# First expert stage in units of 256 rows, with stationary weights loaded for each unit

## The reference

```python
logits = xf @ Wg.T + bg                         # xf: layer norm of x, (4096, 256)
tp, ti = top_k(softmax(logits), 2)
tp = tp / (sum(tp) + 1e-8)
h = gelu(einsum('td,efd->tef', xf, W1) + b1)    # 8 experts, 256 -> 1024
y = einsum('tef,edf->ted', h, W2) + b2          # 1024 -> 256
x + einsum('ted,te->td', y, w)                  # w: tp at the two chosen experts
```

## Time and profile before

| | us |
|---|---|
| median of three runs | 1426.46 |
| the profiled execution's own time | 1424.49 |
| its span | 1422.7 |
| TensorE busy | 1353.1 (95%) |
| VectorE busy | 925.7 (65%) |
| ScalarE busy | 759.3 (53%) |
| GpSimd busy | 380.5 (27%) |
| first expert stage, first up product to the next stage's first product | 359.88 to 840.30 |

### The profile page before, as it was taken

One profiled execution on the slowest core, in us unless ns is written; L12 is line 12 of the kernel. 1 busy time (PEld: TensorE's weight loads), 2 busy tenths in 40 slices (PEclk: granted clock), 3 DMA queues, 4 the chain that ended last, 5 costly groups with the idle time before them and its releaser, 6 DMA issues.

```text
span 1422.7 us, 39700 instructions
## 1 busy us (share of the span) xinstructions
PE 1353.1 (95%) x14238; PEld 1164.5 (82%) x14238; DVE 925.7 (65%) x2570; ACT 759.3 (53%) x1734; POOL 380.5 (27%) x476
## 2 busy tenths in 40 slices
PE   7999999997899999999999989999999999899898
PEld 5888888885799999999999977889899898645476
DVE  4889999876555555555555545888888886412287
ACT  3666666562555555555555543565565655332353
POOL 1344444444030303031230013433344331100131
PEclk9999999997899999999999996999999999999999
DMA  5765445453321212122121111451111110399912
GB/s 185 278 221 171 158 156 171 143 184 118 138 98 38 105 38 97 43 101 97 43 101 39 38 50 38 174 188 47 46 47 57 50 39 17 129 390 428 357 63 67
DMA packets 95481, 175.98 MB, mean 124 GB/s; under 512 B 9024, under 2 KB 85568, under 8 KB 90688
## 3 DMA queue, kind: packets, MB, share of 16 engines
q1 hardware_dynamic: 88288, 144.09, 28.3%
q0 software_dynamic: 7008, 29.37, 6.0%
HBM read 112.87 MB, written 60.56 MB: 122 GB/s over the span
## 4 chain that ended last, share of the span: by engine, by line
PE 78%; DVE 13%; issue 3%; DMA 3%; ACT 2%; POOL 0%; SPq 0%; ACTq 0%; DVEq 0%; PEldq 0%; POOLq 0%
PE ps L1269 14%; PE ps L1254 7%; PE psS L519 4%; PE psS L1254 4%; PE ps L685 3%; PE psT L1254 3%; PE psT L528 3%; PE ps L545 3%; PE ps L551 3%; PE ps L640 3%; DVE arena L919 3%; PE ps L625 2%; PE ps L652 2%; PE psT L1237 2%; PE ps L1237 2%
## 5 line engine op out<-in xcount | busy, mean ns | idle before, releaser
L528 PE MATMUL psT<-arena 32*128 32x128 f32 x2048 | 151.5, 286 | 0.1
L519 PE MATMUL psS<-arena 32*128 32x256 f32 x1024 | 142.7, 397 | 0.7 <-ACT arena L797 0.7
L1269 PE MATMUL ps<-ring_hi,hT_hi 128*128 (+1 forms) x568 | 139.0, 283 | 0.4 <-ACT hT_hi L1282 0.4
L1269 PE MATMUL ps<-ring_lo,hT_hi 128*128 (+1 forms) x568 | 139.4, 283 | 0.0
L1300 ACT ACTIVATE arena<-arena 128x512 f32<-128x512 f32 x142 | 89.7, 632 | 77.1 <-DVE arena L1327 77.1
L1347 DVE TENSOR_TENSOR arena<-ps,arena 128x256 f32<-128x256 f32 x71 | 30.1, 424 | 154.0 <-PE ps L1269 154.0
L528 PEld LDWEIGHTS psT<-arena 32*128 32x128 f32 x2048 | 126.8, 189 | 1.2 <-issue 1.2
L1269 PEld LDWEIGHTS ps<-ring_hi,hT_hi 128*128 128x128 f32 x568 | 108.4, 191 | 3.4 <-issue 0.7
L1269 PEld LDWEIGHTS ps<-ring_lo,hT_hi 128*128 128x128 f32 x568 | 108.7, 191 | 2.7
L1282 ACT CAST hT_hi<-psT 128x512 fp32r<-128x512 f32 x71 | 41.7, 587 | 129.1 <-PE psT L1237 129.1
L919 DVE TENSOR_REDUCE arena<-psS 128x8 f32<-128x1024 f32 x64 | 78.4, 1224 | 44.6 <-PE psS L519 44.6
(11 more groups left out here) (295 smaller groups left out, 3686.7 us busy)
## 6 DMA issues: line engine op xcount, KB each, us to landing
arena<-wset_dram SPq DMA_DIRECT2D x24, 2048.0 KB, 15.2
xs_rows<-arena SPq DMA_DIRECT2D x32, 1024.0 KB, 5.9
arena<-w_dram POOLq DMA_DIRECT2D x6, 2048.0 KB, 9.0
w_sb<-xs_rows SPq DMA_DIRECT2D x71, 128.0 KB, 2.0
xs_rows<-arena SPq DMA_DIRECT2D x71, 128.0 KB, 1.7
arena<-ctxT_dram SPq DMA_DIRECT2D x63, 128.0 KB, 2.2
x_all<-x_dram SPq DMA_DIRECT2D x32, 128.0 KB, 2.1
arena<-w_dram SPq DMA_DIRECT2D x2, 2048.0 KB, 11.9
```

What stands on the lines that cost most here:

```text
L519: last = nc.tensor.matmul(psS[:, b, c * D:(c + 1) * D], qT[p, k % 3, c, :], kbd[p, k % 3, c, :, :], start=A, stop=A or c == 1, skip_group_ ...
L528: nc.tensor.matmul(psT[:, b, j * P:(j + 1) * P], kbd[p, (k - 1) % 3, c, par, :], qT[p, (k - 1) % 3, c, :], start=j == 0, stop=False, skip_ ...
L1269: last = nc.tensor.matmul(ps[5][:, 0:D], hp[:, f, :], wp[:, bass.ds(ring[j - 1], 1), o:o + D], start=n == 0 and f == 0 and wp is ring_hi, ...
```

## The change

The stage runs 33 units of 256 rows (pairs) and then 6 of 128 rows (singles). Routing makes the table in two parts: 33 pairs in `routing` and the six singles in `lone_units`, which VectorE runs in unit 1.

In a pair the weights are stationary and 256 tokens move, so that the up products come out transposed (1024 hidden features in eight groups of 128, two to a PSUM bank). ScalarE adds `b1` as the bias of gelu, straight from PSUM into `hid`. VectorE copies `hid` to `hT_hi` and subtracts into `hT_lo`, bank by bank. No hidden tile is transposed. Every pair loads its expert's weights, in two halves of 1 MB, into one of two slots; ScalarE rounds them in four pieces of 1024 columns between its gelus, and GpSimd subtracts in two instructions of 128x2048. `wb_lo` lies on the place of `wb_raw`. A single loads its weights whole (2 MB) into one of four places and multiplies in plain fp32: 16 up products of 128 columns and 8 down products of 256.

In `attention(0)` only expert 0's weights are prepared, in pieces of 256 columns (before: two experts, pieces of 512). The loads of `b1` to all partitions, the VectorE bias add, `cend_i`, and the reset of `vz` at the stage's end are gone; the context loads for `attention(1)` are issued at the start of the stage.

```diff
-UNITS = 2 * B + E0 - 1
-RING = 2
+PAIRS, SINGLES = B + 1, 6
+UNITS = PAIRS + SINGLES
+WROW = E0 + 4 * 1024
...
                     if A and 8 <= k < 24:
-                        i, o = (k - 8) // 8, (k - 8) % 8 * 512
-                        nc.scalar.copy(ring_hi[:, i, o:o + 512], ring_raw[:, i, o:o + 512]).then_inc(first_hi, 1)
+                        o = E0 + (k - 8) * 256
+                        nc.scalar.copy(wb_hi[:, 0, o:o + 256], wb_raw[:, 0, o:o + 256]).then_inc(first_hi, 1)
...
+            def sync(sp):
+                for u in range(UNITS):
+                    if u == 2:
+                        sp.wait_ge(ones_v.sem, ones_v.at(0, "unit_e"))
+                    if ok(u + 3):
+                        sp.wait_ge(x_p.sem, x_p.at(u + 1, "x"))
+                        rows_in(u + 3)
+                    if pair(u + 2):
+                        e = expert(u + 2)
+                        sp.wait_ge(ge_a.sem, ge_a.at(u, "b3"))
+                        sp.dma_start(wb_raw[:, u % 2, 0:FC + C * F0], ...).then_inc(ld_w1[u % 2], 16)
+                        sp.wait_ge(dn_p.sem, dn_p.at(u, "y"))
+                        sp.dma_start(wb_raw[:, u % 2, FC + C * F0:], ...).then_inc(ld_w2[u % 2], 16)
...
             def gpsimd(pool):
+                for u in range(1, PAIRS):
+                    for n, part in enumerate((slice(FC, FC + C * F0), slice(FC + C * F0, WROW))):
+                        pool.wait_ge(w_a.sem, w_a.at(u - 1, f"w{n + 1}"))
+                        nc.gpsimd.tensor_tensor(wb_lo[:, u % 2, part], wb_raw[:, u % 2, part], wb_hi[:, u % 2, part],
+                                                ALU.subtract).then_inc(w_g.sem, 1)
...
+                def up_pair(u):
+                    pe.wait_ge(w_g.sem, w_g.at(u - 1, "w1"))
+                    pe.wait_ge(x_a.sem, x_a.at(u, "hi"))
+                    for f in range(FC):
+                        if f % 2 == 0:
+                            before(pe, ge_a.sem, ge_a.at(u - 1, f"b{f // 2}"))
+                        o = f % 2 * 2 * P
+                        for n, (wp, xp) in enumerate(((hi, xT_hi), (lo, xT_hi), (hi, xT_lo))):
+                            for c in range(C):
+                                last = nc.tensor.matmul(ps[1 + f // 2][:, o:o + 2 * P], wp[:, c, f * P:(f + 1) * P],
+                                                        xp[:, c, :], start=n == 0 and c == 0, stop=n == 2 and c == C - 1)
+                        if f % 2 == 1:
+                            last.then_inc(up_p.sem, 1)
+
+                def down_pair(u):
+                    pe.wait_ge(w_g.sem, w_g.at(u - 1, "w2"))
+                    before(pe, y_v.sem, y_v.at(u - 1, "y"))
+                    for f in range(FC):
+                        if f % 2 == 0:
+                            pe.wait_ge(h_v.sem, h_v.at(u, f"lo{f // 2}"))
+                        for t in range(2):
+                            for n, (hp, wp) in enumerate(((hT_hi, hi), (hT_hi, lo), (hT_lo, hi))):
+                                last = nc.tensor.matmul(ps[5][:, t * D:(t + 1) * D], hp[:, f, t * P:(t + 1) * P], wp[:, f, :], ...)
+                    last.then_inc(dn_p.sem, 1)
...
+                for u in range(UNITS):
+                    if pair(u):
+                        up_pair(u)
+                    else:
+                        up_single(u)
+                    if ok(u + 1):
+                        turned(u + 1)
+                    if pair(u):
+                        down_pair(u)
+                    else:
+                        down_single(u)
...
             def scalar(act):
+                for u in range(UNITS):
+                    for b in range(4):
+                        act.wait_ge(up_p.sem, up_p.at(u, f"b{b}"))
+                        for f in (2 * b, 2 * b + 1):
+                            last = nc.scalar.activation(hid[:, f, 0:n], ps[1 + b][:, f % 2 * n:f % 2 * n + n], ACT.Gelu,
+                                                        bias=bias[:, f:f + 1])
+                        last.then_inc(ge_a.sem, 1)
+                        if u > 0 and pair(u + 1) and b < 2:
+                            rounded_half(u + 1, 0, b)
+                    if ok(u + 1):
+                        tokens_out(u + 1)
+                    if pair(u + 1):
+                        rounded_half(u + 1, 1, 0)
+                        rounded_half(u + 1, 1, 1)
...
             def vector(dve):
+                        for b in range(4):
+                            dve.wait_ge(ge_a.sem, ge_a.at(u, f"b{b}"))
+                            nc.vector.tensor_copy(hT_hi[:, 2 * b:2 * b + 2, :], hid[:, 2 * b:2 * b + 2, :]).then_inc(h_v.sem, 1)
+                            dve.wait_ge(h_v.sem, h_v.at(u, f"hi{b}"))
+                            nc.vector.tensor_tensor(hT_lo[:, 2 * b:2 * b + 2, :], hid[:, 2 * b:2 * b + 2, :],
+                                                    hT_hi[:, 2 * b:2 * b + 2, :], ALU.subtract).then_inc(h_v.sem, 1)
+                    if pair(u + 1):
+                        tokens_rest(u + 1)
```

More of the change, by code:

```diff
@@ L32 @@
 ROWS_EACH = TOKENS
-SPARE = E0 - 1
+SPARE = SINGLES + 2
 DUMP = E0 * ROWS_EACH
@@ L1058, in attention @@
             return sync, tensor, scalar, vector, gpsimd
-        route_v = track("route_v", "first blk n end wait dst cmp prod uexp pick least unit_s unit_e ex", 1)
+        route_v = track("route_v", "cnt blk n pairs least1 least odd whole odds fit more use sum end comp each dst prod uexp "
+                        "pick low unit_s unit_e ex", 1)
+        ones_v = track("ones_v", "twice left sum cmp step span dst prod uexp pick low at base unit_s unit_e", 1)
         route_a = sem("route_a")
@@ new lines, in pair, with tokens, single, first @@
+            def pair(u):
+                return 0 <= u < PAIRS
+            def tokens(u):
+                return 2 * P if pair(u) else P
+            def single(u):
+                v = u - PAIRS
+                b = 1 - v // 2 % 2
+                return 2 * (v // 2 % 2) + v % 2, (wb_32 if v % 2 else wb_raw)[:, b, :]
+            def first(w):
+                return w[:, FC:FC + C * F0].rearrange("p (c f) -> p c f", c=C)
+            def second(w):
+                return w[:, FC + C * F0:].rearrange("p (f d) -> p f d", f=FC)
@@ new lines, in up_single @@
+                def up_single(u):
+                    slot, wr = single(u)
+                    pe.wait_ge(ld_one[slot], 16 * ((u - PAIRS) // 4 + 1))
+                    pe.wait_ge(x_a.sem, x_a.at(u, "off"))
+                    for f in range(FC):
+                        if f % 2 == 0:
+                            pe.wait_ge(ge_a.sem, ge_a.at(u - 1, f"b{f // 2}"))
+                        o = f % 2 * P
+                        for c in range(C):
+                            last = nc.tensor.matmul(ps[1 + f // 2][:, o:o + P], first(wr)[:, c, f * P:(f + 1) * P],
+                                                    xoff[:, c, 0:P], start=c == 0, stop=c == C - 1)
+                        if f % 2 == 1:
+                            last.then_inc(up_p.sem, 1)
@@ new lines, in down_single @@
+                def down_single(u):
+                    slot, wr = single(u)
+                    pe.wait_ge(y_v.sem, y_v.at(u - 1, "y"))
+                    for f in range(FC):
+                        if f % 2 == 0:
+                            pe.wait_ge(ge_a.sem, ge_a.at(u, f"b{f // 2}"))
+                        last = nc.tensor.matmul(ps[5][:, 0:D], hid[:, f, 0:P], second(wr)[:, f, :],
+                                                start=f == 0, stop=f == FC - 1)
+                    last.then_inc(dn_p.sem, 1)
@@ new lines, in vector @@
+                for u in range(UNITS):
+                    e = expert(u) if u else 0
+                    if pair(u):
+                        for b in range(4):
[6 more added lines that the diff above has]
+                        tokens_rest(u + 1)
+                    if u == 1:
+                        lone_units(dve)
+                    weights(dve, u)
+                    n = tokens(u) // P
+                    dve.wait_ge(dn_p.sem, dn_p.at(u, "y"))
+                    if u == 0:
+                        dve.wait_ge(ld_b2, 16)
+                    before(dve, st_ys[u % 2], 16 * (u // 2))
+                    nc.vector.tensor_tensor(yb[:, u % 2, 0:n, :], ps[5][:, 0:n * D].rearrange("p (t d) -> p t d", t=n),
+                                            b2_sb[:, bass.ds(e, 1), :].to_broadcast([P, n, D]), ALU.add).then_inc(y_v.sem, 1)
```

489 lines of the change are left out of this document (240 added, 249 removed).

## The result

The changed kernel takes 1623.71 us, the median of 4 runs (1623.57 to 1625.18), beside 1425.66 for the kernel before in as many: a ratio of 1.139, interval 1.137 to 1.141. The profiled execution has a span of 1621.8 us against 1422.7.

The account below looks back on a forecast made before the run. TensorE bounds the kernel before; VectorE blocked by GpSimd was to stretch pairs. Unit 1 at 377.2, 31 pairs at 19.0 (589), last pair 12, singles 43.5: next stage at 1021.7, +181.4, so 1605.9 us; range 1465 to 1660.

Parts of the forecast that it names:

- the forecast's: Expert stage: each GpSimd subtraction blocks VectorE's SBUF copies and two-tile subtractions throughout; 18.0 to 20 us a pair, chance 0.70.
- Rival 1: Expert stage: long GpSimd operations let VectorE through, pairs 11.95 us, 1387 (merely sharing: 1402); chance 0.19 with sharing.
- Rival 2: Expert stage: hold is whole, but VectorE gets bank 3 in before GpSimd's second half; 14.8 us a pair, 1476; chance 0.06.
- Rival 3: Expert stage: the weights' loads bind; 13.1 us a pair at 8 us a half, 15 at 9; 1424 to 1484; chance 0.05.
- Routing: Before the stage: the new chain of VectorE steps takes 6.3 us, +1.5 us, with the first up product at about 361.3.
- unit 1: Start of the stage: its up products wait for two roundings and GpSimd's subtraction of its weights, and start at 377.2.
- GpSimd's half: GpSimd's subtraction of 128x2048 weights: half of 9.04 and its fixed part, 4.6 us.
- the holds alone: Steady pair in the stage: waits for GpSimd's two subtractions make it 18.0 us, not 11.95, before any clock loss.
- ones_v chain: Small VectorE steps in units 1 to 5: costed at nothing, under GpSimd's hold anyway; up to 5 us if not.
- the clock's: TensorE's clock falling behind its two waits a pair: 1.0 us a pair, between bounds of nothing and 1.44.
- The end: End of the stage: costed at nothing, since the same gather follows the last store and the keys need no wait.
- with all of it 1621: The sum with the whole clock loss counted gives 1621; with no clock loss 1575.

Follow-up runs that it names:

- e1: Changed kernel with gelu of a pair writing the hidden tile to two PSUM banks in turn, VectorE splitting from there: 1377.78 us, 0.9685 of the kernel before.
- e2: Changed kernel with VectorE subtracting the weights in four pieces of 1024 columns a pair, no GpSimd work in the stage: 1376.15 us, ratio 0.9682 to the kernel before.
- e5: Changed kernel with VectorE's copy of the hidden tile replaced by a tensor_reduce maximum over an axis of length one: 1578.92 us, one run.
- e4: Changed kernel with 12 and 28 unused TensorE products ahead of the down products of banks 2 and 3 in pairs 1 to 31: 1577.82 us, one run.
- e6: Changed kernel with GpSimd subtracting in pieces of 1024 columns, four a pair instead of two of 2048: 1556.49 us, one run.
- e3: Changed kernel with GpSimd subtracting in pieces of 512 columns, eight a pair instead of two of 2048: 1428.62 us, one run.

## Why the prediction was right

**The mechanism** was the forecast's and no rival's. Rival 1 (no hold) falls with copies of 4.80 us; e1 and e2, which take the hold away, show what it priced at 1387: 1376 to 1378. Rival 2's condition came up by half: bank 3's copy got in ahead in 7 of the 30 steady pairs, but its subtraction was held then, as the forecast says, and bank 3 was ready only 0.1 us sooner. Rival 3: the halves of the weights landed in 5.8 and 5.9 us (6.0 said), and e1 took them at 11.8 us a pair.

The Trainium skill's rule, "SBUF — State Buffer", section "Who interferes with whom" (the other engine blocks fully, for the whole instruction), agrees with this trace for GpSimd instructions of 4.66 us. The same section says that tensor_reduce never contends on this chip; e5 agrees, with 689 ns at most.

**The steps that hold.** Routing +1.2 us (+1.5 said), first up product at 361.81 (361.3), unit 1 at 377.95 (377.2), GpSimd's half 4.66 (4.6), a single 7.25 (7.25). That the start came out to 0.5 us is in part luck: in the six other runs, with the same code up to there, it lies between 359.5 and 364.3. With the holds alone a pair takes 17.93 (18.0). The ones_v chain ran from 396.11 to 398.79, in unit 1, and VectorE still stood for 0.22 us behind it, waiting for the down products: it cost nothing, as said.

**The term that was mis-sized** is the clock's. I took 1.0 us a pair, from bounds of 0 and 1.44, the last quarter of the down products at half speed. Measured are 1.8 in the mean, and up to 2.4 in the longest pairs (20.3 against 17.9): the upper bound was too low as well. The low level doesn't end with that quarter: it lasts into the next pair's up products (653.42 and some 3 us on), so that the first gelu, ScalarE's roundings and GpSimd's first half come later too, 6.3 us behind the pair's first product (633.39 to 639.73) instead of the 5.4 of the working, and of 5.15 in e4. From first up product to first up product the 31 pairs take 19.69 each, 0.69 over 19.0; that is 21.4 us, and 0.75 from the start and 0.8 from the last pair and the singles make the next stage's 1044.6 of 1021.7. In the sum "with all of it 1621" 31 times 1.44 gives 1619.5; nothing hangs on that.

**The end**, costed at nothing, went the other way by 5.2 us; without it the forecast would have been 23 us low instead of 18. A part is seen where four products of the last attention ran at half clock before (L659), and not after (L660):

```profile
1225.32 2.02 PE L659 MATMUL ps<-w_sb,x_all 128*128 128x256 f32 x4 [0.55 <-ACT arena L792]
...
1231.45 0.71 PE L666 MATMUL ps<-arena 128*128 128x128 f32 x4 [0.95 <-ACT arena L792]
```

```profile
1428.93 1.10 PE L660 MATMUL ps<-w_sb,x_all 128*128 128x256 f32 x4 [0.55 <-ACT arena L793]
...
1433.39 0.71 PE L667 MATMUL ps<-arena 128*128 128x128 f32 x4 [0.61 <-ACT arena L793]
```

From the first of these rows to the second it is 6.13 us before and 4.46 after, 1.67 less. Of the rest, 0.7 lie ahead of them and 2.8 behind; their cause is open. The change touches no code of the last stages. The kernel before alone takes between 1419.85 and 1426.59 us from run to run, so a difference of 5 us between two single executions can't be put down to the change. In the other changed kernels the same part takes 577.0 to 577.7 us, and 581.6 in e4.

## What to carry to other kernels

Before work goes to a second engine, look where its operands and those of its neighbour lie: a long GpSimd instruction on SBUF puts off VectorE's copies and two-tile operations until it ends, and with them all that stands behind. Moving one operand to PSUM, or giving VectorE all of the work, took that away here and makes the change 3.2% faster than the kernel before (e1, e2); cutting the long instruction helps less than it seems to, because each short operation can meet a piece of its own (pieces of 4.66 us: 19.7 a pair, 2.5: 17.5, 1.5: 13.3). And a wait of 3.6 us on TensorE costs more than itself, because what follows runs at half clock and delays what it feeds.

## What the runs showed of the hardware that I had not expected

The two engines take turns, one instruction each, and by 0.1 us in who comes first a pair falls into one of two lengths, 15.2 or 19.0 (e6). It isn't without exception: in e3 one copy of the 132, at 380.19, took 2.68, over the end of more than one piece. TensorE's clock cost 1.8 us a pair with waits of some 1.6 and 3.6 us, more than the half speed of the products right behind them. And ScalarE's gelu into PSUM and VectorE's 0.69 for the copy from there, beside 0.42 within SBUF, cost the path nothing (e1).
